# First feed-forward of an eight-stage kernel: the first product on quantised integers in bf16, the token scales applied by VectorE behind it, the convolution one slot later

## The reference, cut to what matters

```python
def act_quant(x):
    scale = 127.0 / jnp.clip(jnp.max(jnp.abs(x), axis=-1, keepdims=True), 1e-05)
    return jnp.clip(jnp.round(x * scale), -128, 127) / scale
def weight_quant(w):
    scale = 1.0 / jnp.clip(jnp.mean(jnp.abs(w)), 1e-05)
    return jnp.clip(jnp.round(w * scale), -1, 1) / scale
h = bit_linear(x, w1)                      # 256 -> 1024
h = depthwise_conv1d(h, conv_w, conv_b)    # 3 taps along the tokens
h = silu(h)
return bit_linear(h, w2)                   # 1024 -> 256
```

## Time and profile before

| | us |
|---|---|
| median of 3 runs | 1992.68 (1990.23 to 1996.04) |
| the profiled execution's own time | 1990.66 |
| its span, first to last instruction | 1988.7 |
| TensorE matmuls busy | 1665.2 (84% of the span) |
| VectorE busy | 1147.6 (58%) |
| ScalarE busy | 886.7 (45%) |
| mean granted TensorE clock | 0.92 |

### The profile page before, as it was taken

How to read it: one execution, slowest core, us unless ns; L and a number is a source line. 1 busy time by engine, 2 the same in 40 slices (tenths; PEclk the granted TensorE clock), 3 DMA queues, 4 the chain that set the end, 5 groups by cost and what they waited for, 6 DMA issues and landing times. The chain is left out here.

```text
span 1988.7 us, 30162 instructions
## 1 busy us (share of the span) xinstructions
PE 1665.2 (84%) x10213; PEld 1281.5 (64%) x10213; DVE 1147.6 (58%) x2495; ACT 886.7 (45%) x1809; POOL 321.3 (16%) x359
## 2 busy tenths in 40 slices
PE   6894678885789997789997669999953999969998
PEld 4452345555567665588886659999942888854446
DVE  5664567774445556789886653322246889852115
ACT  2333567664433221256663245555543566623223
POOL 0000000000000002211110055555552111001110
PEclk9897799998889998899998569999986999989999
DMA  5001000003000000100001912222252000010002
GB/s 150 1 1 43 0 0 1 1 0 114 1 1 1 1 1 9 29 1 1 2 2 53 389 54 73 73 70 73 73 163 67 1 1 1 1 46 0 1 0 85
DMA packets 64798, 78.80 MB, mean 40 GB/s; under 512 B 15131, under 2 KB 54607, under 8 KB 64271
## 3 DMA queue, kind: packets, MB, share of 16 engines
q1 hardware_dynamic: 46711, 49.20, 7.5%
q0 software_dynamic: 7584, 20.72, 3.2%
q10 hardware_dynamic: 10360, 7.01, 1.1%
HBM read 58.17 MB, written 18.74 MB: 39 GB/s over the span
## 5 line engine op out<-in xcount | busy, mean ns | idle before, releaser
L2778 PEld LDWEIGHTS moe_bank<-moe_xt,moe_w1e 128*128 128x128 f32 x1264 | 155.1, 194 | 5.8 <-DVE moe_xt L2636 1.9
L2778 PE MATMUL moe_bank<-moe_xt,moe_w1e 128*128 128x128 f32 x1264 | 155.8, 277 | 1.1 <-DVE moe_xt L2636 1.1
L2788 PE MATMUL moe_bank<-moe_w,moe_xin 128*128 x632 | 149.4, 380 | 0.0
L2839 ACT ACTIVATE moe_xin<-moe_bank,moe_b 128x128 f32<-128x128 f32 x316 | 90.5, 368 | 124.3 <-PE moe_bank L2778 124.2
L376 PE MATMUL l0f_hb<-l0f_xt,l0f_w 128*128 128x512 f32 x256 | 125.2, 620 | 5.6 <-DVE l0f_a L307 3.8
L1078 POOL TENSOR_TENSOR all_x<-all_x,l1f_bias 128x256 f32 x32 | 23.1, 724 | 648.1 <-DVE l1f_xn L190 648.1
L2788 PEld LDWEIGHTS moe_bank<-moe_w,moe_xin 128*128 128x128 f32 x632 | 114.1, 190 | 12.2
L195 DVE BATCH_NORM_STATS2 all_stats<-all_x 128x6 f32<-128x256 f32 (+1 forms) x256 | 104.1, 422 | 8.4
L2645 DVE TENSOR_TENSOR moe_y<-moe_bank,moe_b2r 128x256 f32<-128x256 f32 x79 | 33.6, 425 | 118.4 <-PE moe_bank L2788 118.4
L2705 POOL DMA_INDIRECT moe_results<-moe_y,moe_row x79 | 78.0, 988 | 125.2 <-DVE moe_y L2645 121.9
L2636 DVE COPY moe_xt<-moe_bank 128x256 f32<-128x256 f32 x79 | 33.6, 425 | 107.0 <-PE moe_bank L2766 107.0
(11 more groups left out here) (468 smaller groups left out, 3796.7 us busy)
## 6 DMA issues: line engine op xcount, KB each, us to landing
moe_w<-in_L_ffn_W SPq DMA_DIRECT2D x32, 512.0 KB
moe_w<-moe_results SPq DMA_DIRECT2D x16, 512.0 KB, 8.9
all_x<-in_x SPq DMA_DIRECT2D x4, 1024.0 KB, 14.1
out_x<-all_x SPq DMA_DIRECT2D x8, 512.0 KB, 2.9
l0f_w<-in_L_ffn_w_T SPq DMA_DIRECT2D x2, 1024.0 KB
moe_inputs<-moe_xin ACTq DMA_DIRECT2D x16, 128.0 KB, 5.6
moe_inputs<-moe_w1e ACTq DMA_DIRECT2D x16, 128.0 KB, 5.2
moe_b2r<-in_L_ffn_b SPq DMA_DIRECT2D x1, 2048.0 KB, 11.6
```

The costliest lines, as they stand in the source:

```text
L2778: ins = nc.tensor.matmul(out, w1e[:, at:at + P], xt[:, u, c * P:(c + 1) * P], start=(c == 0), stop=(c == DC - 1))
L2788: ins = nc.tensor.matmul(bank[4 + u][:, 0:D], ht[:, u, c * P:(c + 1) * P], w2[:, ds(e * (HC * D) + c * D, D)], start=(c == 0), stop=(c == ...
L2839: ins = nc.scalar.activation(ht[:, u, m * P:(m + 1) * P], bank[1 + u][:, m * P:(m + 1) * P], ACT.Gelu, bias=b1[:, ds(e * HC + m, 1)])
```

## The change

- `turn_x` now turns the quantised values with MAGIC still in them, and `copy_x` subtracts MAGIC and writes bf16 integers. `dequantise` is gone. `w1q` is the ternary weight in bf16, so `up` is a bf16 product.
- The factor `inv1` of each token is now a column factor of the product. `turn_scales` (TensorE) multiplies a broadcast of each `inv1` column by the identity, which puts the 128 values of a token tile in a row in all partitions of `back`, four tiles at a time; `copy_scales` (ScalarE) copies them to `irow`. That happens twice per batch: before the first slot, and in slots m = 4 and m = 5 for the next batch, between `turn_x` and `down` on TensorE.
- `scaled` (VectorE) multiplies the product in PSUM by `irow` into a new SBUF buffer `hs` of three. `centre` and the taps read `hs`.
- In slot g, `scaled` and `centre` take block g-1, and the taps and `silu` take block g-2. `LAG` is 10. The quantisation of w2 moves from slot 2 to 3.
- `up` waits for `scaled` two blocks back, where it waited for the taps.

```diff
-    LAG = M + 1
+    LAG = M + 2
...
-        xt = s.sb("xt", [P, 2, DC, S])
+        xt = s.sb("xt", [P, 2, DC, S], BF16)
+        irow = s.sb("irow", [P, 2, S])
+        hs = s.sb("hs", [P, 3, S])
...
-                def dequantise(t):
-                    j = t % TB
-                    dve.wait_ge(s.q1_ready, t + 1)
-                    nc.vector.tensor_scalar(xn[:, j, :], xn[:, j, :], MAGIC, inv1[:, j:j + 1], ALU.subtract, ALU.mult).then_inc(s.xd_ready, 1)
...
+                def scaled(g):
+                    dve.wait_ge(s.h_ps, g + 1)
+                    if g >= 3:
+                        dve.wait_ge(s.conv_ready, g - 2)
+                    if g % M == 0:
+                        dve.wait_ge(s.irow_ready, 2 * (g // M) + 2)
+                    nc.vector.tensor_tensor(hs[:, g % 3, :], hb[g % 2][:, :], irow[:, g // M % 2, :], ALU.mult).then_inc(s.hs_ready, 1)
...
                     if 1 <= g <= SLOTS:
-                        conv(g - 1, 0)
-                        conv(g - 1, 1)
-                    if b < B - 1 and m >= HM:
-                        dequantise((b + 1) * TB + 2 * (m - HM))
-                        dequantise((b + 1) * TB + 2 * (m - HM) + 1)
+                        scaled(g - 1)
+                    if 2 <= g <= SLOTS + 1:
+                        conv(g - 2, 0)
+                        conv(g - 2, 1)
...
+                def turn_scales(b, half, fed, quantised):
+                    pe.wait_ge(s.insc_ready, b + 1)
+                    pe.wait_ge(s.xt_ready, fed)
+                    pe.wait_ge(s.q2_ready, quantised)
+                    pe.wait_ge(s.irow_ready, 2 * b + half)
+                    for j in range(HM):
+                        at = half * HM + j
+                        ins = nc.tensor.matmul(back[:, j * P:(j + 1) * P], inv1[:, at:at + 1].to_broadcast((P, P)), sh.ident[:, :],
+                                               start=True, stop=True)
+                    ins.then_inc(s.irow_ps, 1)
...
-                            pe.wait_ge(s.conv_ready, g - 1)
+                            pe.wait_ge(s.hs_ready, g - 1)
...
-                        turn_x(fed, max(0, 2 * t))
+                        turn_x(fed, max(0, 2 * t), turned)
                         fed += 2
+                        if m < HM + 2:
+                            turn_scales(b + 1, m - HM, fed, max(0, 2 * t))
+                            turned += 1
                     if 0 <= t - 1 < T:
                         down(t - 1)
...
+                def copy_scales(b, half):
+                    act.wait_ge(s.irow_ps, 2 * b + half + 1)
+                    if b >= 2:
+                        act.wait_ge(s.hs_ready, (b - 1) * M)
+                    nc.scalar.activation(irow[:, b % 2, half * 512:(half + 1) * 512], back[:, :], ACT.Copy).then_inc(s.irow_ready, 1)
...
-                    act.wait_ge(s.h_ps, g + 1)
+                    act.wait_ge(s.hs_ready, g + 1)
...
-                    nc.scalar.activation(a[:, u, :], hb[g % 2][:, :], ACT.Identity, scale=cw[:, m, 1:2], bias=cb[:, m:m + 1]).then_inc(s.a_ready, 1)
+                    nc.scalar.activation(a[:, u, :], hs[:, g % 3, :], ACT.Identity, scale=cw[:, m, 1:2], bias=cb[:, m:m + 1]).then_inc(s.a_ready, 1)
...
-                    if 1 <= g <= SLOTS:
-                        silu(g - 1)
+                    if 2 <= g <= SLOTS + 1:
+                        silu(g - 2)
...
                     if b < B - 1 and m >= HM:
                         copy_x((b + 1) * TB + 2 * (m - HM))
+                        if m < HM + 2:
+                            copy_scales(b + 1, m - HM)
```

More of the change, by code:

```diff
@@ L214, in stage_l0_ffn @@
         w1, w2 = s.sb("w1", [P, DC, HID]), s.sb("w2", [P, M, D])
-        w2q = s.sb("w2q", [P, M, D], BF16)
+        w1q, w2q = s.sb("w1q", [P, DC, HID], BF16), s.sb("w2q", [P, M, D], BF16)
         wsum, wscale, wmean = s.sb("wsum", [P, 2]), s.sb("wscale", [P, 2]), s.sb("wmean", [P, 2])
@@ L231, in stage_l0_ffn @@
         for n in ["w_loaded", "small_loaded", "wsum_ready", "wtot_ps", "wscale_ready", "w1_ready", "w2_scaled", "w2_ready", "table_loaded",
-                  "rstd_ready", "norm_ready", "step", "insc_ready", "q1_ready", "xd_ready", "xt_ps", "xt_ready", "h_ps", "a_ready",
+                  "rstd_ready", "norm_ready", "step", "insc_ready", "q1_ready", "irow_ps", "irow_ready", "xt_ps", "xt_ready", "h_ps", "hs_ready", "a_ready",
                   "conv_ready", "z_ready", "am2_step", "sc2_ready", "inv2_ready", "zt_ps", "zq_ready", "back_ps", "q2_ready", "y_ps",
@@ L273, in input_scales @@
                     if b:
-                        dve.wait_ge(s.xd_ready, b * TB)
+                        dve.wait_ge(s.q1_ready, b * TB)
+                        dve.wait_ge(s.irow_ps, 2 * b)
                     nc.vector.tensor_scalar(inv1[:, :], am[:, :], wmean[:, 0:1], None, ALU.mult)
@@ L294, in _ @@
                 c.link(nc.vector.tensor_scalar(w1[:, :, :], w1[:, :, :], MAGIC, 1.0, ALU.subtract, ALU.min))
-                nc.vector.tensor_scalar(w1[:, :, :], w1[:, :, :], -1.0, None, ALU.max).then_inc(s.w1_ready, 1)
-                for t in range(TB):
-                    dequantise(t)
+                nc.vector.tensor_scalar(w1q[:, :, :], w1[:, :, :], -1.0, None, ALU.max).then_inc(s.w1_ready, 1)
                 dve.wait_ge(s.small_loaded, 32)
+                def scaled(g):
[5 more added lines that the diff above has]
+                    nc.vector.tensor_tensor(hs[:, g % 3, :], hb[g % 2][:, :], irow[:, g // M % 2, :], ALU.mult).then_inc(s.hs_ready, 1)
                 def conv(g, tap):
                     m, u = g % M, g % 3
-                    h = hb[g % 2]
+                    h = hs[:, g % 3, :]
                     if tap == 0:
@@ L347, in _ @@
                         stats(t - 2)
-                    if g == 2:
+                    if g == 3:
                         dve.wait_ge(s.w2_scaled, 1)
@@ L357, in _, with turn_x @@
                 nc.tensor.matmul(yb[:, 0:2], sh.ones[:, :], wsum[:, :], start=True, stop=True).then_inc(s.wtot_ps, 1)
-                def turn_x(t, quantised):
+                def turn_x(t, quantised, turned):
                     pe.wait_ge(s.xt_ready, t)
                     pe.wait_ge(s.q2_ready, quantised)
-                    pe.wait_ge(s.xd_ready, t + 2)
+                    pe.wait_ge(s.q1_ready, t + 2)
+                    pe.wait_ge(s.irow_ready, turned)
                     for i in range(2):
@@ L373, in up @@
                         if g >= 2:
-                            pe.wait_ge(s.conv_ready, g - 1)
+                            pe.wait_ge(s.hs_ready, g - 1)
                     for d in range(DC):
-                        ins = nc.tensor.matmul(hb[g % 2][:, half * 512:(half + 1) * 512], w1[:, d, m * P:(m + 1) * P],
+                        ins = nc.tensor.matmul(hb[g % 2][:, half * 512:(half + 1) * 512], w1q[:, d, m * P:(m + 1) * P],
                                                xt[:, b % 2, d, half * 512:(half + 1) * 512], start=(d == 0), stop=(d == DC - 1))
@@ L386, in turn_z @@
                         if last_in_z(t) is None:
-                            pe.wait_ge(s.conv_ready, SLOTS)
+                            pe.wait_ge(s.hs_ready, SLOTS)
                         else:
@@ L393, in turn_z, with turn_back @@
                     ins.then_inc(s.zt_ps, 1)
-                def turn_back(t, half, fed):
+                def turn_back(t, half, fed, turned):
                     pe.wait_ge(s.zq_ready, 2 * t + half + 1)
@@ L422, in _ @@
                 for t in range(0, TB, 2):
-                    turn_x(t, 0)
-                fed = TB
+                    turn_x(t, 0, 0)
+                fed, turned = TB, 2
+                turn_scales(0, 0, fed, 0)
+                turn_scales(0, 1, fed, 0)
                 pe.wait_ge(s.w1_ready, 1)
@@ L432, in _ @@
                     if 0 <= t - 1 < T:
-                        turn_back(t - 1, 0, fed)
+                        turn_back(t - 1, 0, fed, turned)
                     if g < SLOTS:
@@ L436, in _ @@
                     if 0 <= t - 1 < T:
-                        turn_back(t - 1, 1, fed)
+                        turn_back(t - 1, 1, fed, turned)
                     if 0 <= t <= TAIL:
@@ L479, in copy_x @@
                     nc.scalar.activation(xt[:, b % 2, :, j * P:(j + 2) * P].rearrange("p c (t n) -> p t c n", n=P),
-                                         back[:, :].rearrange("p (t c n) -> p t c n", t=2, n=P), ACT.Copy).then_inc(s.xt_ready, 2)
+                                         back[:, :].rearrange("p (t c n) -> p t c n", t=2, n=P), ACT.Copy, bias=-MAGIC).then_inc(s.xt_ready, 2)
+                def copy_scales(b, half):
[3 more added lines that the diff above has]
+                    nc.scalar.activation(irow[:, b % 2, half * 512:(half + 1) * 512], back[:, :], ACT.Copy).then_inc(s.irow_ready, 1)
                 def centre(g):
                     m, u = g % M, g % 3
-                    act.wait_ge(s.h_ps, g + 1)
```

(5 more changed lines are left out.)

## The result

| | before | after |
|---|---|---|
| median of runs, us | 1992.28 (1990.23 to 1996.04, 4 runs) | 2024.94 (2024.01 to 2029.09, 4 runs) |
| ratio to before, 95% interval | | 1.0166 (1.0145 to 1.0187) |
| profiled execution, its span | 1990.66, 1988.7 | 2024.01, 2021.9 |
| TensorE, VectorE, ScalarE busy | 1665.2, 1147.6, 886.7 | 1633.3, 1174.3, 891.6 |
| mean granted clock | 0.92 | 0.90 |

The change makes the kernel 1.7% slower, 33 us. The direction was forecast, and 2024.9 lies inside the range of 1980 to 2028, but the forecast of 2006 has less than half of the loss: it said +14.

A forecast was written before the change was run, and what follows sets the result against it. It took a ring of ScalarE, VectorE, ScalarE as the bound of the plain step, with TensorE missing it by half a microsecond. 1990.66 - 4.0 + 6.9 + 13 = 2006.6, stated as 2006 us, range 1980 to 2028.

The forecast's parts named there:

- Before the first step: Feed-forward stage ahead of its first reduction L312: that reduction comes at 264.05 instead of 268.10 us, -4.0 us.
- The walk: Slots 1 to 10 followed by known durations to place each `scaled` and the first reduction; good to some 3 us.
- The steps at full clock: The 24 steps between reductions in the first feed-forward stage: 181.2 us against 174.26, +6.9 us.
- The kinds: Step types: L269 ahead 7.53, `input_scales` 8.31, turned scales 10.29, `copy_x` and `quantise_x` 7.26, plain 6.82, no `scaled` 5.29 us.
- The clock: TensorE at 1.2 GHz in 10 of the 24 steps, 1.29 us more each: +13 us.
- the upper bound: All 24 steps at the low clock, 31 us, and near 7 more in four steps with turned scales: 38 us.
- the new ring: Plain step: `scaled`, `centre`, `copy_q`, `turn_back`, `turn_z`, reduction, each waiting for the last; 6.82 us against 6.55.
- the taps' wait: VectorE in the kernel before: L305 idles 0.88 us until `centre` L487 ends.
- two stalls per batch at the turned scales: Slots m=4 and m=5: `update`, then `scaled`, wait for `down` queued behind `turn_scales`; almost 2 us each.
- A: Rival: TensorE's clock holds at 2.4 GHz in the stage; +2.9 us, 1993.6 us; chance 0.17.
- B: Rival: transposes don't keep TensorE's clock up, so it stays at 1.2 GHz; +41 us, 2032 us; chance 0.13.
- C: Rival: the reduction's new wait does not form, VectorE's work bounds; -15 us, 1975.6 with the clock high; chance 0.14.

The follow-up runs named there:

- e1: The changed kernel with the first product back in f32 (`w1q` and `xt` in f32), all else as changed: 2021.75 us, ratio to before 1.0152.
- e4: The changed kernel with the first `copy_q` moved ahead of `centre` in ScalarE's queue: 1997.49 us, ratio to before 1.0014.
- e8: The changed kernel with `copy_q` ahead of `centre`, `down` ahead of `turn_scales`, and eight unused bf16 products per step: 1988.29 us, ratio to before 0.9980.
- e6: The kernel before with only `w1q` and `xt` in bf16, not keeping exactness: 1997.32 us, ratio to before 1.0013.
- e5: The changed kernel with both orders: first `copy_q` ahead of `centre`, and `down` ahead of `turn_scales`: 1986.83 us, ratio to before 0.9968.
- e2: The changed kernel with eight unused bf16 products of 256 columns behind the first half of `up`: 2013.89 us, ratio to before 1.0100.

## Why the prediction was right in kind and wrong in size

The difference between the profiled 2024.0 and the summed 2006.6 is 17.4 us. By the prediction's own steps:

- **Before the first step.** -4.0 forecast, -2.1 measured. The walk put `scaled` of slot 0 at 217.45 and of slot 9 at 260.4; they started at 218.01 and 262.31, with the two waits for `up` where it had them. Off by +1.9.
- **The steps at full clock.** +6.9 forecast. The kinds were 7.53, 8.31, 10.29, 7.26, 6.82 and, for the last two, 5.29. Measured are 7.69, 8.47, 10.55 (from e1), 7.43, 6.97 and 5.32 (from e1). 8.47 is an estimate: the one step of the kernel after, 9.76, less the 1.29 more that its reduction waits at the low clock (2.18 against 0.89). The first two steps are shorter than their kinds, 6.96 and 8.15 in e1, for no `stats` stand in them yet, and in the first no `update` either; the prediction had counted them. That makes 6.96 + 8.15 + 3 x 7.69 + 8.47 + 4 x 10.55 + 2 x 7.43 + 10 x 6.97 + 2 x 5.32 = 184.1, so +9.8, off by +2.9. In the plain steps the cause is one duration: `centre` from SBUF takes 1.24, not the 1.05 that L493 gave, and `copy_q` starts 1.15 behind it, not 0.94. L493 was the wrong neighbour. It is a ScalarE pass of the same shape and source, but another function, without a scale and a bias of its own per partition; L487, the same operation from PSUM, 1.21, was the nearer row.
- **The clock, +13 forecast.** 205.75 - 184.1 = 21.7 measured, off by +8.7. This is the step of the prediction that failed: the term of the clock in the sum. It priced every step at the low clock alike, 10 x 1.29. Of the 21.7, the four steps with turned scales hold 8.8 (13.24, 13.44, 11.81 and 12.47 against 4 x 10.55), 2.2 each, and the last two 3.5 (7.07 and 7.06 against 2 x 5.32), 1.7 each; the other eighteen hold 9.4. The steps with the longest stalls are also those whose TensorE work waits longest and then runs at the low clock, and they carry eight more records of `turn_scales` (2.05 at 287.16, where 1.04 was walked). The prediction named 7 us for them, but in the upper bound alone.
- **Not forecast at all.** +3.5 in the next cross-attention and +0.4 elsewhere. Whether the +3.5 is a consequence of the change stays open: over the runs that stage took 292.3 to 297.7 with no order that I can see, 297.7 in e4 and 292.3 in e8.

1.9 + 2.9 + 8.7 + 3.5 + 0.4 = 17.4.

What held: that TensorE's busy time does not set the step (e6), where the new ring stands (L514 released by L302, L316 by L407, L326 by L435), that the taps' wait goes, and two stalls per batch at the turned scales. That the two orders are the cause of the loss is shown by e4 and e5. The clock's share of the steps is worked out from rows of two runs and not measured apart, and e2 supports it from the side: a filler wins 10.1 us of it back.

The rivals: A, the clock holds, is refuted by 0.82. B, low throughout, is refuted too: many steps take 6.97 with `turn_z` at 1.04. Its 2032 was nearer to the result than my 2006, by the wrong road: the clock took 21.7 us, not 38, and the steps at full clock and the next stage made up for part of that. C, that the wait does not form, is refuted as forecast for this kernel, and e5 shows what it would have been worth: 5.99 per step. I priced C at 0.81 off 6.82, which is 6.01.

The Trainium skill, "TensorE: Matmul & The Clock Gate", section "Why this matters for your kernels", had spoken for A by its rule on idle gaps between bursts, as the prediction gives it. The trace disagrees: idle stretches of 2.68 us ahead of 330.89 and 1.12 ahead of 386.73 in e6 were followed by the low clock. The same page's Part 4, by which transposes do not count as busy in the same way, would have led to a low clock in all plain steps, as rival B had it; most of them here ran at full clock, seven of ten.

The prediction also said that no gap would be as long as that rule allows. Two were longer than its 2.7: TensorE idled 3.13 us ahead of 280.83 and 3.45 us ahead of 356.67, in the two steps with `input_scales`.

## What to carry to other kernels

When an operation is put between a producer and a consumer, walk each queue it stands in: what sits behind the newly delayed instruction (here `copy_q` behind `centre`, `down` behind `turn_scales`) decides the time, and moving one call ahead of it can be worth more than the change. A cheaper matmul on an engine that is off the ring buys nothing (e6), and if it was the work that held TensorE's clock up, its steps get longer where the clock falls; price the low clock by kind of step, the stalled ones highest. Count the slots ahead of the first result as well as the steady steps.

## What the hardware did that I had not expected

- An idle stretch of the same length, 2.68 and 2.67 us, was followed by the low clock at 330.89 and by the full clock at 339.78, with the same two groups right ahead of it. In e6 the clock fell after idle stretches of 1.53 and 1.12 us. The length of one gap did not decide it.
- Eight bf16 products per step with no use (e2) raised the clock of the steps from 0.82 to 0.93 and made the kernel some 13 us faster.
- ScalarE's pass with a scale and bias per partition gained nothing by reading SBUF: 1.240 in 32 instances, against 1.201 from PSUM in e6.
